# Bending the graph part with features on partitions: transposes in place of the second products

## The chip, the cores and the metric

The kernel runs on one core of a Trainium2 chip. The metric is device time in microseconds (us) from start to end of the program. An ordinary stretch of this kernel uses five engines at once: TensorE (products and transposes), VectorE, ScalarE, GpSimd and SyncE, which only issues transfers. They meet at semaphores. On-chip memory has 128 partitions. TensorE writes its results to a small separate memory (PSUM, here ps0 to ps7), from which VectorE and ScalarE read.

## The reference, cut to what matters

There are 6250 nodes with 256 features and 100,000 edges. The output is `x + gnn + mix` and a mixture-of-experts part on top. The change touches only the graph part (gnn), whose sums over edges are multiplied with W, shifted and scaled by statistics over all nodes and features, and bent with a leaky slope:

```python
xn = _layernorm(x, axis=-1)
# _L0_gnn_ref(xn, ...)
h = x @ W                                  # 6250 x 256 by 256 x 256
deg = jax.ops.segment_sum(jnp.ones_like(dst_f, dtype=h.dtype), dst_f, num_segments=n)
dinv = jax.lax.rsqrt(deg)
norm = dinv[src_f] * dinv[dst_f]
out = jax.ops.segment_sum(h[src_f] * norm[:, None], dst_f, num_segments=n) + conv_bias
mu = out.mean()
xc = out - mu
std = jnp.sqrt((xc * xc).mean())
y = xc / (std + EPS) * ln_weight + ln_bias
return jnp.where(y >= 0, y, prelu_a * y)
# then
x = x + gnn(xn) + mix(xn)
x = x + ffn(_layernorm(x, axis=-1))        # 8 experts, the best two of each row
```

## The kernel before

The program is a sequence of phases with a barrier behind each.

1. Statistics, degrees, a scaled table of rows in DRAM (to about 138 us).
2. Aggregation (140 to 789 us, groups `q` of edges). It sums table rows over edges with one-hot products, and runs the attention part between. The sums lie in `acc` with the 256 features on partitions (two halves `k` of 128) and the nodes along the row: `acc[:, k, node]`. At its end, SyncE loads the last weights (lines 725 to 731), and x tiles and table rows (lines 710, 716, 718) stand before them in its queue. `o_tile(t)` (in R2) holds x plus the attention result for tile t, features of both halves side by side, nodes on partitions.
3. The router phase (789 to 972 us), where the change lies. It works on T = 49 tiles of 128 nodes.
   - First pass: `rows(t)` on TensorE (line 1456) turns a tile of `acc` into 128 nodes by 256 features with two products by W (`gw`). VectorE scales it by `dinv` of each node and adds the bias (line 1615) and takes its statistics (1620).
   - Totals: VectorE joins the statistics (1639 to 1656) and asks TensorE twice for sums over partitions (1472, 1473). ScalarE takes a root (1536). VectorE multiplies W by the final scale of each feature (`wx`, line 1665).
   - Second pass: `scaled(t)` on TensorE (1482) repeats the two products, now by `wx`. VectorE scales by `dinv` and adds the shift (1675). ScalarE takes the negative part (1542), GpSimd adds the value into `o_tile` (1588). VectorE adds the negative part times 1 - slope (`finish`, 1681), and takes row statistics (1686, 1690). TensorE turns the finished tile (`flip`, 1491), ScalarE copies it (1548), TensorE multiplies it with the 8 router columns (`logits`, 1498).
   - Behind it, VectorE turns the statistics into scales (1704 to 1712) and chooses the experts (from 1724 on). ScalarE writes normalised rows (1564). One-hot products find each row's place (1526).
4. Experts (972 to 1377 us).

Each engine runs its own list in the order written. In the second pass TensorE's step s is `scaled(s)`, `flip(s - 4)`, `logits(s - 5)`; VectorE's is `shifted(s)`, `x_stats(s - 3)`, `x_stats_joined(s - 4)`, `finish(s - 2)`. SyncE stores each four finished tiles (`store_x1`, waits for `x_ok`) and loads expert weights over parts of `acc` that are done with (`load_w2`, waits for `px_ok`).

A float32 product is two instructions in the trace, a float32 transpose one.

Of the kernel before, what the change touches and what calls it, by code (L numbers as in the profile page):

```python
# [7 lines left out]
P = 128  # L8
# [47 lines left out]
W1ROW = KC * HID + HC  # L56


def build(nc, a_x, a_src, a_dst, a_gw, a_cb, a_lnw, a_lnb, a_pre, a_wqkv, a_mk, a_mv, a_wout, a_bout,
# [4 lines left out]
    ntable = nc.dram_tensor("ntable", (N, D + 2), f32, kind="Internal").ap()  # L64
    with ExitStack() as ctx:
# [34 lines left out]
        dslow = R1[:, 0:NC].rearrange("p (g c) -> p g c", c=GC)  # L100
        gw = RG[:, 4 * D:6 * D].rearrange("p (k n) -> p k n", k=KC)
        cbias, lnw, lnb = (RG[:, k * D:(k + 1) * D] for k in (6, 7, 8))
# [28 lines left out]
        pre = sb("pre", [P, 1])  # L131
        brr = sb("brr", [P, NX])
# [524 lines left out]
        with nc.Block(no_gpsimd_drain=True) as block:  # L657
# [43 lines left out]
            late = semaphore(phase, "a_late_weights_in")  # L701

            @block.sync
            def _(sp):
# [27 lines left out]

# [13 lines left out]
            def _(pe):  # L746
# [86 lines left out]
                def attention(q, r):  # L833
# [23 lines left out]
                    if q == C1 + 2 and r == 2:  # L857
                        pe.wait_ge(mid_dve, 5)
                        nc.tensor.matmul(psO, cnT, wout[:, :], start=True, stop=True).then_inc(mid_pe, 1)
                        pe.wait_ge(mid_dve, 6)  # L860
                    for s in quarter(share(q, B0, B1, T + 3), r):
# [102 lines left out]
            def _(v):  # L964
# [117 lines left out]
                def attention(q, r):  # L1082
# [61 lines left out]
                    if q == B1 + 1 and r == 0:  # L1144
# [6 lines left out]
                                                               ALU.mult))  # L1151
                    for t in quarter(share(q, D0, D1, T), r):
# [133 lines left out]
        aw, a1 = slot[:, 2, :], small[:, 20:21]  # L1286
        tot2, share_of = small[:, 24:26], small[:, 48:50]
        wx = RG[:, 0:2 * D].rearrange("p (k n) -> p k n", k=KC)
        bx = RG[:, 2 * D:3 * D]
# [61 lines left out]
        with nc.Block(no_gpsimd_drain=True) as block:  # L1351
            pr_ok = semaphore(phase, "r_products")
            y_ok = semaphore(phase, "r_rows_ready")
# [6 lines left out]
            sh_ok = semaphore(phase, "r_shares")  # L1360
            wx_ok = semaphore(phase, "r_scaled_weights")
            px_ok = semaphore(phase, "r_scaled_products")
            v_ok = semaphore(phase, "r_shifted")
            ng_ok = semaphore(phase, "r_negative_part")
# [698 lines left out]
```

## Time and profile before

| what | value |
|---|---|
| median of 3 runs | 1373.95 us |
| the three runs | 1378.43, 1372.21, 1373.95 us |
| profiled execution | span 1377.2 us from its first to its last instruction; its own time is not listed apart |
| TensorE, VectorE busy | 1245.3 us (90%), 962.4 us (70%) |
| ScalarE, GpSimd busy | 539.3 us (39%), 854.3 us (62%) |
| mean granted TensorE clock | 0.960 of full speed |

PE is TensorE's products and PEld its loads of the stationary operand, DVE is VectorE, ACT ScalarE, POOL GpSimd and SP SyncE. A `q` behind an engine's name is its sequencer. PEclk is the granted clock of TensorE as a share of 2.4 GHz: it has two levels, 0.50 and 1.00, and a value between is a stretch with both. A matmul's recorded duration contains its way through the array, so that the distance from start to start tells what it costs in a stream.

### The profile page before, as it was taken

Reading aid. Unit: us, or ns where it says so; the run is one execution under the profiler, and the core shown is the slowest. Engines: PE = TensorE matmul, PEld = TensorE weight load, DVE = VectorE, ACT = ScalarE, POOL = GpSimd, SP = SyncE. Lnnn points to the kernel's source line nnn. Section 1 sums busy time; section 2 is a strip of 40 time slices with the busy share of each in tenths; the row PEclk is TensorE's granted clock in tenths of the full one; section 3 lists DMA queues with packets and bytes.
Section 4 is the critical chain, followed back from the end, with each engine's and each line's share of the span. In section 5 each row is a group of like instructions: output and inputs, shape, how many; then the busy total and the mean of one; then the engine's idle time right before and its main releaser. Section 6 shows DMA issues by size and latency. Waiting matters only on the chain. (4 is left out here: it accounts for less than half of the span.)

```text
span 1377.2 us, 30864 instructions
## 1 busy us (share of the span) xinstructions
PE 1245.3 (90%) x8354; PEld 1106.3 (80%) x8355; DVE 962.4 (70%) x2966; ACT 539.3 (39%) x1443; POOL 854.3 (62%) x836
## 2 busy tenths in 40 slices
PE   4997688999899999999898797985799999999998
PEld 4984687887788888887787686873699999999997
DVE  8998787887888777778693288998444444444444
ACT  7707301222333333333311101446455555555553
POOL 1294677777777777777777202431376666666665
PEclk9999899999999999999999898995799999999999
DMA  7005333335666666789898400449244444444443
GB/s 245 0 0 183 111 106 103 107 105 172 194 194 199 198 191 202 207 246 277 260 288 261 144 1 16 138 155 318 64 77 66 68 71 69 72 69 70 71 69 42
DMA packets 138148, 186.89 MB, mean 136 GB/s; under 512 B 21438, under 2 KB 116468, under 8 KB 137916
## 3 DMA queue, kind: packets, MB, share of 16 engines
q0 software_dynamic: 43440, 90.29, 28.7%
q1 hardware_dynamic: 94604, 95.40, 21.8%
q8 instruction: 42, 0.69, 0.2%
q14 instruction: 62, 0.51, 0.1%
HBM read 153.16 MB, written 33.41 MB: 135 GB/s over the span
## 5 line engine op out<-in xcount | busy, mean ns | idle before, releaser
L740 POOL DMA_INDIRECT RG<-table,srci x484 | 477.3, 986 | 153.0 <-issue 149.4
L757 PEld LDWEIGHTS ps<-S_t,RG 128*128 128x128 f32 x1936 | 259.2, 196 | 39.0 <-DMA RG<-table,srci 28.6
L757 PE MATMUL ps<-S_t,RG 128*128 128x96 f32 x1936 | 266.4, 278 | 21.6 <-DMA RG<-table,srci 21.1
L780 PE MATMUL ps<-zrow,R 128*128 128x256 f32 (+1 forms) x784 | 221.1, 389 | 15.2 <-DMA zrow<-table 8.7
L2010 POOL DMA_INDIRECT out<-R,S_t x105 | 166.3, 1584 | 99.5 <-DVE R L1980 55.8
L1893 PE MATMUL ps<-R,RG 128*128 128x128 f32 x1680 | 207.3, 277 | 0.0
L1893 PEld LDWEIGHTS ps<-R,RG 128*128 128x128 f32 x1680 | 198.3, 194 | 0.4 <-issue 0.4
L1903 PE MATMUL ps<-R 128*128 x840 | 198.5, 379 | 0.0
L1014 DVE TENSOR_TENSOR R<-R,ps 128x245 f32 (+4 forms) x300 | 142.1, 474 | 73.7 <-PE ps L768 52.5
L1926 ACT ACTIVATE R<-ps,RG 128x128 f32<-128x128 f32 x420 | 120.0, 368 | 175.8 <-PE ps L1893 175.8
L1976 DVE TENSOR_TENSOR R<-ps,R 128x256 f32<-128x256 f32 x105 | 44.6, 425 | 200.8 <-PE ps L1903 200.8
L780 PEld LDWEIGHTS ps<-zrow,R 128*128 128x128 f32 (+1 forms) x784 | 136.9, 192 | 41.2 <-DMA zrow<-table 19.8
L1903 PEld LDWEIGHTS ps<-R 128*128 128x128 f32 x840 | 151.7, 190 | 16.3
L884 ACT ACTIVATE R<-iwin 128x256 f32<-128x256 f32 (+2 forms) x152 | 71.3, 476 | 186.0 <-PE ps L780 174.2
L1998 POOL DMA_INDIRECT R<-ntable,S_t x105 | 104.2, 992 | 41.5 <-issue 29.0
L1935 ACT ACTIVATE RG<-R 128x1028 f32 x105 | 112.8, 1076 | 10.6 <-PEq L76 10.6
L1588 POOL TENSOR_TENSOR R<-R,slot 128x256 f32<-128x256 f32 x49 | 35.9, 733 | 93.5 <-DVE slot L1675 93.5
L455 PE MATMUL ps<-R 128*128 128x49 bf16 x784 | 80.7, 276 | 10.4 <-DVE R L544 10.3
L455 PEld LDWEIGHTS ps<-R 128*128 128x128 bf16 x784 | 72.7, 144 | 18.4 <-DVE R L544 12.2
L1965 DVE TENSOR_SCALAR R<-ps,gamma,beta 128x128 f32<-128x128 f32 x212 | 76.1, 400 | 0.0
L971 DVE TENSOR_TENSOR S_t<-dstrel,iwin 128x384 f32<-128x384 f32 x121 | 66.7, 551 | 0.7
L984 DVE TENSOR_TENSOR R<-R,ps 128x192 f32 x121 | 42.7, 353 | 31.0 <-issue 23.4
(360 smaller groups left out, 1989.9 us busy)
## 6 DMA issues: line engine op xcount, KB each, us to landing
zrow<-table SPq DMA_DIRECT2D x384, 128.0 KB
RG<-table,srci POOLq DMA_INDIRECT x484, 3.3
ntable<-R SPq DMA_DIRECT2D x12, 516.0 KB
table<-RG SPq DMA_DIRECT2D x12, 512.0 KB, 2.9
out<-R SPq DMA_DIRECT2D x12, 512.0 KB, 3.2
R<-in_x SPq DMA_DIRECT2D x6, 896.0 KB, 11.7
R<-in_w SPq DMA_DIRECT2D x8, 514.0 KB, 6.4
slot<-in_x SPq DMA_DIRECT2D x32, 128.0 KB
```

Source lines behind the costliest of these rows:

```text
L455: last = nc.tensor.matmul(ps[7][:, 0:T], ohlo[k][:, :, c], ohhi[k][:, :, c], start=False, stop=False)
L740: nc.gpsimd.indirect_dma_start(out=grows[:, s, :], out_offset=None, in_=table, in_offset=bass.IndirectOffsetOnAxis(ap=srci[:, ND + q, c:c ...
L757: last = nc.tensor.matmul(window(q % 2)[:, h, :], grows[:, s, h * P:(h + 1) * P], S_t[:, q % 2, c, :], start=c == 0, stop=c == GC - 1)
L780: nc.tensor.matmul(psD[:, 0:D], adj[b % 2][0:n, j, :], zrow[0:n, i % ZR, :], start=j == 0, stop=j == T - 1).then_inc(z_used, 1)
L1014: nc.vector.tensor_tensor(win, win, psK[m % 2][:, 0:T * wide].rearrange("p (j w) -> p j w", w=wide), ALU.add).then_inc(cnt_ok, 1)
L1893: last = nc.tensor.matmul(psH[s % 2][:, h * P:(h + 1) * P], w1r[:, s, k * HID + h * P:k * HID + (h + 1) * P], ur[:, s % 2, k, :], start=k ...
L1903: last = nc.tensor.matmul(psY[s % 2][:, 0:D], hr[:, s % 2, h, :], w2_sb[:, bass.ds(e, 1), h, :].rearrange("p a f -> p (a f)"), start=h == ...
L1926: last = act.activation(hr[:, s % 2, h, :], psH[s % 2][:, h * P:(h + 1) * P], ACT.Gelu, bias=w1r[:, s, KC * HID + h:KC * HID + h + 1])
L1935: act.activation(w1r[:, s, :], w1_sb[:, bass.ds(e, 1), :].rearrange("p a f -> p (a f)"), ACT.Copy).then_inc(c_ok, 1)
L1965: nc.vector.tensor_scalar(ur[:, s % 2, k, :], psX[s % 2][:, k * P:(k + 1) * P], gamma[:, k:k + 1], beta[:, k:k + 1], ALU.mult, ALU.add)
L1998: nc.gpsimd.indirect_dma_start(out=xr[:, t % 4, :], out_offset=None, in_=ntable, in_offset=bass.IndirectOffsetOnAxis(ap=gat[:, t:t + 1], a ...
L2010: nc.gpsimd.indirect_dma_start(out=a_out, out_offset=bass.IndirectOffsetOnAxis(ap=sct[:, t:t + 1], axis=0), in_=yr[:, t % 4, :], in_offset ...
```

## The change

The order of work behind the aggregation is turned round. W is applied once, in the form that leaves the features on partitions, and the value that comes out replaces the sums in `acc`.

- The row of all `dinv` is needed on every partition. TensorE transposes `dinv` late in the aggregation, it is stored to DRAM as `dflat` (25 KB), and one transfer spreads it to `dall`, 128 partitions of 25,000 bytes each (3.2 MB). It may be issued once the seventh block has been turned, since `dall` lies over that block's counts.
- First pass: `features(i)`, 26 pieces (13 spans of 500 nodes, the last of 250, by 2 halves of the features), each of two products with W stationary and the sums moving. VectorE multiplies each by `dall` back into `acc` and takes statistics of each 250 nodes.
- Bias, weight and shift are now a number per partition, loaded as 2 numbers per partition each (three small transfers), instead of rows of 256 spread over the partitions.
- Second pass, in 13 slabs of 512 nodes: ScalarE scales and shifts the lower half in place (`affine`), VectorE bends it with one instruction (`bent`). For the upper half ScalarE makes two slabs, the line with the small slope (`steep`) and the rectified rest, and GpSimd adds them. `back(t)` transposes the tile to nodes on partitions, and `finish(t)` on VectorE adds it to `o_tile(t)` straight from PSUM. The per-tile work of ScalarE and GpSimd of before (1542, 1588), `shifted` (1675) and the joining of row statistics (1690) are gone; the latter is done for all tiles at once behind the pass. `flip` and `logits` stay, two steps behind instead of four.

```diff
@@ -722,13 +735,19 @@
...
+                    if q == B1 + 6:
+                        sp.wait_ge(dr_ok, 1)
+                        sp.dma_start(dflat.rearrange("(t p) -> t p", p=P), ksl[0:T, 0, :]).then_inc(dr_out, 16)
+                sp.wait_ge(dr_out, 16)
+                sp.wait_ge(blk_t, NDB - 1)
+                sp.dma_start(dall, dflat[0:N].unsqueeze(0).to_broadcast([P, N])).then_inc(da_in, 16)
                 sp.wait_ge(pe_done, GQ - 2)
                 sp.dma_start(gw, a_gw.rearrange("(k p) n -> p k n", p=P)).then_inc(late, 16)
-                sp.dma_start(cbias, a_cb.unsqueeze(0).to_broadcast([P, D])).then_inc(late, 16)
-                sp.dma_start(lnw, a_lnw.unsqueeze(0).to_broadcast([P, D])).then_inc(late, 16)
-                sp.wait_ge(pe_done, GQ - 1)
-                sp.dma_start(lnb, a_lnb.unsqueeze(0).to_broadcast([P, D])).then_inc(late, 16)
+                for dest, source in ((cbf, a_cb), (lnwf, a_lnw), (lnbf, a_lnb)):
+                    sp.dma_start(dest[:, :], source.rearrange("(k p) -> p k", p=P),
+                                 allow_slow_non_contiguous=True).then_inc(late, 16)
                 sp.wait_ge(late, 16 * 4)
+                sp.wait_ge(da_in, 16)
...
@@ -1449,38 +1473,42 @@
...
-                def rows(t):
-                    if t >= 4:
-                        pe.wait_ge(y_ok, t - 3)
+                def features(i):
+
+                    j, f = i // KC, i % KC
+                    if i >= 6:
+                        pe.wait_ge(u_ok, i - 5)
+                    lo, hi = j * SPAN, min(j * SPAN + SPAN, N)
                     for k in range(KC):
-                        last = nc.tensor.matmul(ps[t % 4][:, 0:D], acc[:, k, t * P:(t + 1) * P], gw[:, k, :],
+                        last = nc.tensor.matmul(ps[i % 6][:, 0:hi - lo], gw[:, k, f * P:(f + 1) * P], acc[:, k, lo:hi],
                                                 start=k == 0, stop=k == KC - 1)
                     last.then_inc(pr_ok, 1)
 
-                for t in range(4):
-                    rows(t)
+                for i in range(4):
+                    features(i)
                 pe.wait_ge(g_ok, 2)
                 for k in range(KC):
-                    nc.tensor.matmul(ps[5][:, 0:NX], betas[:, k, :], wr[:, k, :], start=k == 0, stop=k == KC - 1)
+                    nc.tensor.matmul(ps[6][:, 0:NX], betas[:, k, :], wr[:, k, :], start=k == 0, stop=k == KC - 1)
                 for k in range(KC):
-                    last = nc.tensor.matmul(ps[6][:, 0:NX], ones[:, :], wrg[:, k, :], start=k == 0, stop=k == KC - 1)
+                    last = nc.tensor.matmul(ps[7][:, 0:NX], ones[:, :], wrg[:, k, :], start=k == 0, stop=k == KC - 1)
                 last.then_inc(g_ps, 1)
-                for t in range(4, T):
-                    rows(t)
+                for i in range(4, KC * NSPAN):
+                    features(i)
                 for n in range(2):
                     pe.wait_ge(part, n + 1)
-                    nc.tensor.matmul(ps[7][:, n:n + 1], ones[:, :], tot2[:, 0:1], start=True, stop=False)
-                    nc.tensor.matmul(ps[7][:, n:n + 1], ones[:, :], tot2[:, 1:2], start=False,
-                                     stop=True).then_inc(whole, 1)
-
-                pe.wait_ge(wx_ok, 1)
-
-                def scaled(t):
+                    for k in range(KC):
+                        last = nc.tensor.matmul(ps[7][:, n:n + 1], ones[:, :], tot2[:, k:k + 1], start=k == 0,
+                                                stop=k == KC - 1)
+                    last.then_inc(whole, 1)
...
+                def back(t):
+                    pe.wait_ge(pr_in, t // 4 + 1)
+                    pe.wait_ge(ps_in, t // 4 + 1)
                     if t >= 2:
-                        pe.wait_ge(v_ok, t - 1)
+                        pe.wait_ge(x_ok, t - 1)
                     for k in range(KC):
-                        last = nc.tensor.matmul(psW[t % 2][:, 0:D], acc[:, k, t * P:(t + 1) * P], wx[:, k, :],
-                                                start=k == 0, stop=k == KC - 1)
+                        last = nc.tensor.transpose(psW[t % 2][:, k * P:(k + 1) * P], acc[:, k, t * P:(t + 1) * P],
+                                                   ident[:, :])
                     last.then_inc(px_ok, 1)
...
@@ -1499,13 +1527,13 @@
...
-                for s in range(T + 5):
+                for s in range(T + 3):
                     if s < T:
-                        scaled(s)
-                    if 0 <= s - 4 < T:
-                        flip(s - 4)
-                    if 0 <= s - 5 < T:
-                        logits(s - 5)
+                        back(s)
+                    if 0 <= s - 2 < T:
+                        flip(s - 2)
+                    if 0 <= s - 3 < T:
+                        logits(s - 3)
...
@@ -1535,11 +1563,17 @@
...
-                def negative(t):
-                    act.wait_ge(v_ok, t + 1)
-                    if t >= 4:
-                        act.wait_ge(x_ok, t - 3)
-                    act.activation(minus[:, t % 4, :], shift[:, t % 4, :], ACT.Relu, scale=-1.0).then_inc(ng_ok, 1)
+                def affine(c):
+                    lo, hi = c * SLAB, min(c * SLAB + SLAB, NP)
+                    act.activation(acc[:, 0, lo:hi], acc[:, 0, lo:hi], ACT.Identity, scale=aw[:, 0:1],
+                                   bias=bw[:, 0:1]).then_inc(af_ok, 1)
+                    if c >= 2:
+                        act.wait_ge(ps_in, c - 1)
+                    act.activation(steep[:, c % 2, 0:hi - lo], acc[:, 1, lo:hi], ACT.Identity, scale=down[:, 0:1],
+                                   bias=down[:, 1:2]).then_inc(lf_ok, 1)
+                    act.wait_ge(lf_ok, c + 1)
+                    act.activation(acc[:, 1, lo:hi], acc[:, 1, lo:hi], ACT.Relu, scale=kink[:, 0:1],
+                                   bias=kink[:, 1:2]).then_inc(kn_ok, 1)
...
@@ -1547,11 +1581,13 @@
...
+                act.wait_ge(fn_ok, 1)
+                for c in range(2):
+                    affine(c)
+                for t in range(T):
+                    if t % 4 == 0 and t // 4 + 2 < NSLAB:
+                        affine(t // 4 + 2)
+                    flipped(t)
...
@@ -1575,20 +1611,17 @@
...
-                def residual(t):
-                    pool.wait_ge(v_ok, t + 1)
-                    nc.gpsimd.tensor_tensor(o_tile(t), o_tile(t), halved(shift[:, t % 4, :]), ALU.add).then_inc(xa_ok, 1)
-
-                for t in range(T):
-                    residual(t)
+                for c in range(NSLAB):
+                    lo, hi = c * SLAB, min(c * SLAB + SLAB, NP)
+                    pool.wait_ge(kn_ok, c + 1)
+                    nc.gpsimd.tensor_tensor(acc[:, 1, lo:hi], acc[:, 1, lo:hi], steep[:, c % 2, 0:hi - lo],
+                                            ALU.add).then_inc(ps_in, 1)
...
@@ -1610,49 +1643,54 @@
...
+                def scaled(j):
+                    lo, hi = j * SPAN, min(j * SPAN + SPAN, N)
+                    v.wait_ge(pr_ok, KC * j + KC)
+                    for f in range(KC):
+                        nc.vector.tensor_tensor(acc[:, f, lo:hi], ps[(KC * j + f) % 6][:, 0:hi - lo], dall[:, lo:hi],
+                                                ALU.mult).then_inc(u_ok, 1)
+
+                def feature_stats(j):
+                    v.wait_ge(u_ok, KC * j + KC)
+                    for f in range(KC):
+                        for i in range(2 * j, min(2 * j + 2, NPIECE)):
+                            last = nc.vector.bn_stats(fstats[:, f, i, :], acc[:, f, i * PIECE:(i + 1) * PIECE])
+                    return last
...
+                for k in range(KC):
+                    last = nc.vector.bn_aggr(both[:, k, :], fstats[:, k, :, :].rearrange("p i s -> p (i s)"))
+                ch.done(last)
+                ch.done(nc.vector.tensor_tensor(tot2, means, cbf[:, :], ALU.add))
...
@@ -1661,46 +1699,48 @@
...
+                ch.done(nc.vector.tensor_tensor(d2, d2, side, ALU.mult))
+                ch.done(nc.vector.tensor_scalar(aw, lnwf[:, :], d2, None, ALU.mult))
+                ch.done(nc.vector.scalar_tensor_tensor(bw, cbf[:, :], mu, aw, ALU.subtract, ALU.mult))
+                ch.done(nc.vector.scalar_tensor_tensor(bw, lnbf[:, :], side, bw, ALU.mult, ALU.add))
+                nc.vector.tensor_tensor(down[:, 0:1], aw[:, 1:2], pre[:, :], ALU.mult)
+                nc.vector.tensor_tensor(down[:, 1:2], bw[:, 1:2], pre[:, :], ALU.mult)
+                nc.vector.tensor_tensor(kink[:, 0:1], aw[:, 1:2], kink[:, 2:3], ALU.mult)
+                ch.done(nc.vector.tensor_tensor(kink[:, 1:2], bw[:, 1:2], kink[:, 2:3], ALU.mult))
+                v.sem_inc(fn_ok, 1)
...
+                def bent(c):
+                    lo, hi = c * SLAB, min(c * SLAB + SLAB, NP)
+                    v.wait_ge(af_ok, c + 1)
+                    nc.vector.scalar_tensor_tensor(acc[:, 0, lo:hi], acc[:, 0, lo:hi], pre[:, 0:1], acc[:, 0, lo:hi],
+                                                   ALU.mult, ALU.max).then_inc(pr_in, 1)
...
+                def finish(t):
                     v.wait_ge(px_ok, t + 1)
-                    if t >= 4:
-                        v.wait_ge(ng_ok, t - 3)
-                        v.wait_ge(xa_ok, t - 3)
-                    nc.vector.scalar_tensor_tensor(shift[:, t % 4, :], psW[t % 2][:, 0:D], dinv[:, t:t + 1], bx, ALU.mult,
-                                                   ALU.add).then_inc(v_ok, 1)
-
-                def finish(t):
-                    v.wait_ge(ng_ok, t + 1)
-                    v.wait_ge(xa_ok, t + 1)
-                    nc.vector.scalar_tensor_tensor(halved(o_all[:, t, :]), halved(minus[:, t % 4, :]), a1, o_tile(t),
+                    nc.vector.scalar_tensor_tensor(halved(o_all[:, t, :]), halved(psW[t % 2][:, 0:D]), side, o_tile(t),
                                                    ALU.mult, ALU.add).then_inc(x_ok, 1)
...
-                def x_stats_joined(t):
-                    v.wait_ge(st_ok, t + 1)
-                    nc.vector.bn_aggr(mv[:, t, :], stats[:, t, :]).then_inc(ag_ok, 1)
...
+                bent(0)
+                for s in range(T + 1):
+                    if s % 4 == 0 and s // 4 + 1 < NSLAB:
+                        bent(s // 4 + 1)
                     if s < T:
-                        shifted(s)
-                    if 0 <= s - 3 < T:
-                        x_stats(s - 3)
-                    if 0 <= s - 4 < T:
-                        x_stats_joined(s - 4)
-                    if 0 <= s - 2 < T:
-                        finish(s - 2)
-                v.wait_ge(ag_ok, T)
-                mean, var = mv[:, :, 0], mv[:, :, 1]
-
+                        finish(s)
+                    if 0 <= s - 1 < T:
+                        x_stats(s - 1)
...
```

On TensorE, around the first pass and the totals in front of the second. `ps` is PSUM, `R` the large buffers (`acc` and the rows), `RG` the weights, `small` a tile of scalars. Before:

```order
L1456 MATMUL ps<-RG,R 128x256 x8
L1464 MATMUL ps<-wr,RG 128x8 x2
L1466 MATMUL ps<-RG,ones 128x8 x2
L1456 MATMUL ps<-RG,R 128x256 x90
L1472 MATMUL ps<-small,ones 128x1
```

After:

```order
L1483 MATMUL ps<-R,RG 128x500 x8
L1491 MATMUL ps<-wr,RG 128x8 x2
L1493 MATMUL ps<-RG,ones 128x8 x2
L1483 MATMUL ps<-R,RG 128x500 x40
L1483 MATMUL ps<-R,RG 128x250 x4
L1500 MATMUL ps<-small,ones 128x1 x4
```

98 products of 256 columns have become 48 of 500 and 4 of 250.

On TensorE in the second pass, from its first instruction on. Before:

```order
L1482 MATMUL ps<-RG,R 128x256 x10
L1491 MATMUL ps<-ident,R 128x128 x2
L1482 MATMUL ps<-RG,R 128x256 x2
L1491 MATMUL ps<-ident,R 128x128 x2
L1498 MATMUL ps<-RG,zrow 128x8 x2
L1482 MATMUL ps<-RG,R 128x256 x2
L1491 MATMUL ps<-ident,R 128x128 x2
L1498 MATMUL ps<-RG,zrow 128x8 x2
```

After:

```order
L1510 MATMUL ps<-ident,R 128x128 x6
L1519 MATMUL ps<-ident,R 128x128 x2
L1510 MATMUL ps<-ident,R 128x128 x2
L1519 MATMUL ps<-ident,R 128x128 x2
L1526 MATMUL ps<-RG,zrow 128x8 x2
L1510 MATMUL ps<-ident,R 128x128 x2
L1519 MATMUL ps<-ident,R 128x128 x2
L1526 MATMUL ps<-RG,zrow 128x8 x2
```

Of a tile's two wide products, two transposes and two narrow products, the wide ones have become transposes.

On ScalarE after, from the first slab on (`zrow` is the turned tile, `slot` the slab `steep`):

```order
L1568 ACTIVATE R<-R,small 128x512
L1572 ACTIVATE slot<-R,small 128x512
L1575 ACTIVATE R<-R,small 128x512
L1568 ACTIVATE R<-R,small 128x512
L1572 ACTIVATE slot<-R,small 128x512
L1575 ACTIVATE R<-R,small 128x512
L1568 ACTIVATE R<-R,small 128x512
L1572 ACTIVATE slot<-R,small 128x512
L1575 ACTIVATE R<-R,small 128x512
L1582 ACTIVATE zrow<-ps 128x256 x4
L1568 ACTIVATE R<-R,small 128x512
```

Three wide instructions now stand in front of each four copies of turned tiles, where before one narrow instruction stood in front of each copy.

## Rows read from the trace of the kernel before

**Rows 1.** The page: TensorE's busy tenths and granted clock in 40 slices.

```profile
PE   4997688999899999999898797985799999999998
...
PEclk9999899999999999999999898995799999999999
```

**Rows 2.** Windows of the router phase: length, busy us by engine, clock, DMA.

```profile
790.00:836.00 46.00, 45.95 (x204) 39.77 (x204) 39.52 (x101) 1.59 (x1) 1.47 (x7) 0.94 0.00 1
...
845.00:920.00 75.00, 74.38 (x462) 66.09 (x463) 71.54 (x186) 32.04 (x92) 35.16 (x48) 0.97 0.36 113
```

**Rows 3.** Timeline of TensorE in the second pass, one tile (start, us, line).

```profile
917.90 0.38 PE L1491 MATMUL ps<-ident,R 128*128 128x128 f32 x2
918.12 0.51 PE L1498 MATMUL ps<-RG,zrow 128*128 128x8 f32 x4
918.49 1.11 PE L1482 MATMUL ps<-RG,R 128*128 128x256 f32 x4
919.43 0.38 PE L1491 MATMUL ps<-ident,R 128*128 128x128 f32 x2
```

**Rows 4.** Timeline of TensorE elsewhere, at the lower clock.

```profile
841.04 0.59 PE L1472 MATMUL ps<-small,ones 128*128 128x1 f32 x2 [1.23 <-DVEq L1652]
841.49 0.56 PE L1473 MATMUL ps<-small,ones 128*128 128x1 f32 x2
...
980.99 0.64 PE L1883 MATMUL ps<-ident,R 128*128 128x128 f32 x2
981.42 2.66 PE L1893 MATMUL ps<-R,RG 128*128 128x128 f32 x16
```

**Rows 5.** Windows where the clock falls, stays low, and rises.

```profile
842.00:844.00 2.00, 0.05 (x1) 0.00 (x0) 1.38 (x8) 0.20 (x1) 0.00 (x0) 0.50 0.00 0
...
850.00:852.00 2.00, 2.00 (x12) 1.68 (x11) 1.89 (x5) 0.84 (x2) 1.32 (x2) 1.00 0.00 0
...
924.00:926.00 2.00, 0.61 (x4) 0.52 (x4) 1.50 (x6) 0.24 (x1) 0.00 (x0) 0.72 1.07 246
...
955.00:960.00 5.00, 5.00 (x27) 3.32 (x24) 4.71 (x6) 3.35 (x8) 1.95 (x2) 0.50 1.05 370
```

**Rows 6.** Timeline: totals, start of the second pass, and its end.

```profile
832.76 3.19 PE L1456 MATMUL ps<-RG,R 128*128 128x256 f32 x14
...
836.39 0.74 DVE L1620 BATCH_NORM_STATS2 RG<-R 128x6 f32<-128x256 f32 x2
837.16 1.45 DVE L1639 BATCH_NORM_AGGREGATE small<-RG 128x2 f32<-128x288 f32 x1
...
844.74 6.66 PEld L1482 LDWEIGHTS ps<-RG,R 128*128 128x128 f32 x20 [2.77 <-DVEq L1666]
...
922.58 0.45 DVE L1681 SCALAR_TENSOR_TENSOR R<-zrow,small,R 128x256 f32<-128x256 f32 x1
...
926.12 0.57 DVE L1724 TENSOR_TENSOR R<-ps,zs_s 128x392 f32<-128x392 f32 x1
```

**Rows 7.** Groups by line: first pass, second pass, wide ScalarE instructions.

```profile
L1615 DVE SCALAR_TENSOR_TENSOR R<-ps,dinv,RG 128x256 f32<-128x256 f32 x49 | 23.7, 483 | 6.4 <-PE ps L1456 4.6
...
L1588 POOL TENSOR_TENSOR R<-R,slot 128x256 f32<-128x256 f32 x48 | 35.2, 733 | 92.7 <-DVE slot L1675 92.7
...
L1935 ACT ACTIVATE RG<-R 128x1028 f32 x105 | 112.8, 1076 | 10.6 <-PEq L76 10.6
L1564 ACT ACTIVATE R<-R,zs_b,zs_s 128x256 f32<-128x256 f32 x49 | 24.8, 588 | 11.4 <-DMA ntable<-R 9.6 <-DVEq L1713 1.8
```

**Rows 8.** Timeline at the end of the aggregation: SyncE's issues, what waits.

```profile
771.34 0.29 SPq L718 DMA_DIRECT2D slot<-in_x  x1
776.82 0.38 SPq L726 DMA_DIRECT2D RG<-in_gw  x1
...
777.66 0.60 ACT L920 ACTIVATE slot<-slot,x1b,x1s 128x256 f32<-128x256 f32 x1 [1.40 <-DMA slot<-in_x]
...
786.06 0.36 DVE L984 TENSOR_TENSOR R<-R,ps 128x192 f32 x1 [2.61 <-PE ps L757]
```

More of the change, by code:

```diff
@@ L131, in build @@
         pre = sb("pre", [P, 1])
+        cbf, lnwf, lnbf = (RG[:, 16 * D + KC * k:16 * D + KC * (k + 1)] for k in range(3))
         brr = sb("brr", [P, NX])
@@ L860, in attention @@
                         pe.wait_ge(mid_dve, 6)
+                    if q == B1 + 1 and r == 0:
+                        pe.wait_ge(qt_ok, T)
+                        nc.tensor.transpose(psT[0:T, :], dinv[:, :], ident[:, :]).then_inc(mid_pe, 1)
                     for s in quarter(share(q, B0, B1, T + 3), r):
@@ new lines, in feature_stats @@
+                def feature_stats(j):
[4 more added lines that the diff above has]
+                    return last
+                scaled(0)
+                for j in range(NSPAN):
+                    if j + 1 < NSPAN:
+                        scaled(j + 1)
+                    if j == 2:
@@ L1627, in _ @@
                         v.wait_ge(g_ps, 1)
-                        ch.done(nc.vector.tensor_tensor(c0, ps[5][:, 0:NX], brr[:, :], ALU.add))
+                        ch.done(nc.vector.tensor_tensor(c0, ps[6][:, 0:NX], brr[:, :], ALU.add))
                         for k in range(KC):
-                            last = nc.vector.scalar_tensor_tensor(wrg[:, k, :], ps[6][:, 0:NX], -1.0 / D, wrg[:, k, :],
+                            last = nc.vector.scalar_tensor_tensor(wrg[:, k, :], ps[7][:, 0:NX], -1.0 / D, wrg[:, k, :],
@@ L1631, in _ @@
                                                                   ALU.mult, ALU.add)
                         ch.done(last)
-                    last = row_stats(t)
+                    last = feature_stats(j)
                 ch.done(last)
-                full = 1.0 / (N * D)
-                pm, tm = small[:, 32:34], small[:, 34:36]
-                means, variances = (small[:, 32:36].rearrange("p (a b) -> p a b", b=2)[:, :, k] for k in range(2))
-                ch.done(nc.vector.bn_aggr(pm, stats[:, 0:T - 1, :].rearrange("p t s -> p (t s)")))
@@ L1640, in _ @@
-                ch.done(nc.vector.bn_aggr(tm, stats[:, T - 1, :]))
-                v.wait_ge(sh_ok, 2)
-                ch.done(nc.vector.tensor_tensor(tot2, means, share_of, ALU.mult))
+                both = small[:, 32:32 + 2 * KC].rearrange("p (k s) -> p k s", s=2)
+                means, variances = both[:, :, 0], both[:, :, 1]
+                for k in range(KC):
+                    last = nc.vector.bn_aggr(both[:, k, :], fstats[:, k, :, :].rearrange("p i s -> p (i s)"))
+                ch.done(last)
@@ L1651, in _ @@
-                ch.done(nc.vector.tensor_tensor(tot2, off, share_of, ALU.mult))
+                ch.done(nc.vector.tensor_tensor(tot2, off, variances, ALU.add))
                 v.sem_inc(part, 1)
@@ L1654, in _ @@
                 val, root = small[:, 31:32], small[:, 30:31]
-                ch.done(nc.vector.tensor_scalar(val, ps[7][:, 1:2], full, 1e-30, ALU.mult, ALU.max))
+                ch.done(nc.vector.tensor_scalar(val, ps[7][:, 1:2], 1.0 / D, 1e-30, ALU.mult, ALU.max))
                 v.sem_inc(root_in, 1)
```

88 lines of the change are left out of this document (43 added, 45 removed).

## The prediction

> **What bounds the kernel now.** I read the page first, from its clock and busy lines: TensorE is busy nearly everywhere, at full clock but for a few dents, the deep one in slices 28 and 29, right behind the passes that the change rewrites (slices 24 to 27) [rows 1]. Then windows by stage. In the first pass of the router phase (790 to 836) TensorE is busy without a break and VectorE for 39.5 of 46 us; in the second (845 to 920) both are full, 74.4 and 71.5 of 75 us [rows 2]. Then TensorE's timeline of one tile in the second pass: a transpose pair to the next pair takes 917.90 to 919.43, 1.53 us, and its parts fill it: 0.22 for two transposes, 0.37 for the narrow products, 0.94 for the wide ones [rows 3]. So both passes hang on TensorE, and their sum is 46 + 78.3 us (844.74 to 922.58 + 0.45, the last `finish`) [rows 6].
>
> The view that decides this case is the clock. TensorE's clock was at 0.50 after the gap (842 to 844), and rose to 1.00 by 850 to 852 under the first twenty 256-column products of the second pass. It fell again in 924 to 926, when the engine had done only transposes and narrow products for the last tiles. And it stayed at 0.50 through 955 to 960, though TensorE was busy 5.00 of 5.00 us with a stream of 105-column bf16 products [rows 5]. Being occupied did not raise it there; wide float32 products did.
>
> **Second pass, the largest term.** The change takes away the wide products, 0.94 us of the 1.53, and puts two transposes there. At full clock a tile is 0.22 + 0.22 + 0.37 = 0.81 us [rows 3]. But the gap before the pass grows: ScalarE and GpSimd must make a slab first, so TensorE stands for some 14 us behind the first pass and starts at 0.50. What it then gets is the very mix that was in front of the fall, transposes and 8-column products, with nothing wide to raise the clock. I expect it to stay at 0.50 for the whole pass. Twice 0.81 is 1.62 us. The rows at 0.50 say directly: two transposes 0.43 (980.99 to 981.42), two narrow instructions 0.45 (841.04 to 841.49), so at most 0.86 + 0.90 = 1.76 [rows 4]. I take 1.65, near the doubled value, because the narrow ones in rows 4 hold a first start; bounds 1.60 and 1.76. 49 x 1.65 = 80.9 us.
>
> Start: ScalarE's 512-column instruction does not occur before. 256 columns with two scalars per partition take 0.588, 1028 plain ones 1.076 [rows 7]; so 512 lie between 0.588 + 256 x (1.076 - 0.588) / 772 = 0.75 and 2 x 0.588 = 1.18. I take 0.8, since the longer row shows how little a column adds. The three of a slab overlap a little, the third waits for the second: 2.4 us to its end. GpSimd's add of 512 is between 0.73 and 1.47 (256 take 0.733 [rows 7]); 1.4. So the first transposes come at 4.0 us after VectorE's flag, where the first wide product now comes at once. The third step waits for the first `finish`, 0.6. Behind the last `back` stand three flips and four sets of narrow products, 3 x 0.43 + 4 x 0.79 = 4.4 us, that the last `finish` does not wait for; transposes and `finish` themselves end 0.9 later. From flag to last `finish`: 4.0 + 0.6 + 80.9 - 4.4 + 0.9 = 82.0 against 78.3: **+3.7 us**, with the bounds of the tile -2.5 and +5.4 around it.
>
> What that hides: VectorE has per four tiles four `finish` (0.48 each by the like L1615 [rows 7]), four statistics (0.37 each by L1620 [rows 6]) and one `bent` of 512, below twice 0.75 even beside GpSimd: under 5 us of 6.6. GpSimd has 1.4 of 6.6. The 98 small instructions taken from ScalarE and GpSimd and the 49 joins on VectorE were beside TensorE and bring nothing. ScalarE is the close one: a slab's three instructions stand in front of each fourth copy, and TensorE cannot pass that copy by more than a step. The circle is slab 2.3, copy 0.37, narrow products 0.8, a whole step 1.65, a `back` and a `flip` 0.86, latencies 0.5: 6.5 us per four tiles against TensorE's 6.6. If TensorE were quicker, this circle would be the bound.
>
> **First pass.** 196 instructions of 256 columns become 96 of 500 and 8 of 250. Fourteen took 3.19 us with the last one's 0.38 [rows 6], so 0.216 apart; 500 columns take 0.42. 41.7 instead of 42.3: -0.6. VectorE has 2 x 0.6 + 4 x 0.34 = 2.6 us per span against TensorE's 3.4, so it stays hidden until the last span. Behind the last product there are now two scalings of 250 and six statistics, 2 x 0.35 + 6 x 0.34 = 2.75, against 1.2 (835.95 to 837.13): +1.6. Joining: 1.45 for 288 values and 0.2 become two of 150 at the same rate, 1.5: -0.15 [rows 6]. Of the small steps behind, the product of W by the scale (0.7) goes and six steps of 0.1 to 0.2 come: 0, within 0.4. **+0.85 us.**
>
> **End of the pass.** Now 3.1 us from the last `finish` to the first step of the choice (923.03 to 926.12 [rows 6]). Joining all statistics at once adds five dependent steps of about 0.25 between them: **+1.2 us**. The last narrow products end 4.0 us behind `finish`, just inside.
>
> **End of the aggregation.** `dall` can be issued right behind the last x tile, at 771.6. 3.2 MB at the 370 GB/s of the busiest window [rows 5] are 8.6 us. The x tile issued at 771.34 landed at 777.66 [rows 8], so some transfer path is late; the part of `dall` behind it would land at 786.3, the weights behind that near 787.5. VectorE's last add ends the phase at 786.42 now [rows 8]. I take **+1.0 us**: hidden altogether is 0, and every transfer in single file about +4. The transpose, the copy and the 25 KB store at group 89 to 94 are nothing beside a whole group's work there.
>
> **Sum.** 3.7 + 0.85 + 1.2 + 1.0 = +6.75 us. The profiled execution's span was 1377.2, inside the three runs (1372.21 to 1378.43); the difference is carried over to their median: 1373.95 + 6.75 = 1380.7, so 1381. A change of 0.5%, 6.9 us, is what I take a measurement to tell from none; the forecast lies on that border.
>
> **Rival 1: the clock comes up.** Then ScalarE's circle binds: 2.3 + 0.37 + 0.4 + 0.81 + 0.43 + 0.4 = 4.7 us, 1.2 per tile. 4.0 + 0.6 + 49 x 1.2 - 2.2 + 0.7 = 61.9, -16.4 against 78.3, with the other terms -13.3: 1361. For it: in 845 to 920 transposes and narrow products ran at full clock between wide ones [rows 2]. Against: rows 5, twice.
> The Trainium skill, TensorE: Matmul & The Clock Gate, section What's actually happening, says that the throttled state is the default and activity releases it, by how busy the engine has been; by that rule TensorE, occupied without a break at 1.65 us per tile, would be released. The trace disagrees in 955 to 960, occupied for 5.00 us at 0.50; 0.16 is what I leave to the rule.
>
> **Rival 2: ScalarE's slabs take TensorE's place.** With 1.18 per wide instruction a slab is 3.4, the circle 7.6 per four tiles, 1.9 per tile: 49 x 0.25 = +12: 1393. It decides from 0.83 per instruction on. For it: two scalars per partition cost at 256 columns more than a plain instruction. Against: 1028 columns in 1.076.
>
> **Rival 3: `dall` and what stands behind it end the aggregation**, about 3 us later than I took: 1384, slower.
>
> **How the numbers follow.** Forecast 0.70, its own range 1376 to 1387, split by the border at 1380.8 into 0.34 below and 0.36 above. Rival 1 0.16 (faster). Rival 2 0.08, rival 3 0.06 (slower). Faster 0.16, same 0.34, slower 0.50. A range of 1373 to 1391 leaves out rival 1 and half of rival 2.
>
> **What would show it.** Right: PEclk 0.50 from the gap to the experts; 1.6 to 1.75 us from pair to pair of `back`; TensorE waiting little, ScalarE less than full; a first transpose 4 us behind the flag; the first pass within a microsecond of its length. Rival 1: PEclk 1.00 in the pass and 1.2 us per tile, TensorE waiting for line 1582. Rival 2: the same wait at 0.50, and line 1568 at 1.1 us. Rival 3: SyncE's last wait ending the aggregation. The forecast is wrong if the clock rises under transposes and narrow products alone, or if transposes at 0.50 run other than 0.21 apart.

## The result, and the profile after

The changed kernel took 1384.62 us (median of 7 runs, 1381.17 to 1386.80) against 1373.95 for the kernel before (7 runs, 1371.16 to 1381.38): ratio 1.0070, 95% interval 1.0049 to 1.0091, so slower by 0.5 to 0.9%. (A ratio is worked out from the single runs of both kernels, so it is not exactly the quotient of the two medians.) The forecast was 1381, 1373 to 1391, slower the likeliest of the three.

The page of the changed kernel, the lines of [rows 1]:

```profile
PE   4997688999899999998898696995799999999998
...
PEclk9999898999999999999999896555799999999999
```

The dent in the clock was two slices long (5, 7) and is now five (6, 5, 5, 5, 7). Above it TensorE reads 6 in the gap and then 9, 9. Windows of the router phase in the changed kernel (columns as in [rows 2]): the first pass, the gap, the second pass.

```profile
791.00:836.00 45.00, 44.69 (x112) 21.05 (x112) 29.82 (x72) 1.61 (x1) 1.30 (x5) 0.96 0.00 0
836.00:851.00 15.00, 2.32 (x10) 2.18 (x11) 9.80 (x36) 4.12 (x7) 1.09 (x1) 0.59 0.00 1
851.00:928.00 77.00, 76.51 (x374) 73.98 (x372) 47.53 (x108) 40.39 (x80) 12.40 (x12) 0.50 0.35 112
```

TensorE stands for most of 15 us, its clock falls, and in the second pass it is busy for 76.51 of 77 us at 0.50. VectorE, full there before, has 30 us to spare. One tile of the second pass, TensorE's timeline of the changed kernel, against [rows 3]:

```profile
902.66 0.67 PE L1510 MATMUL ps<-ident,R 128*128 128x128 f32 x2
903.12 0.64 PE L1519 MATMUL ps<-ident,R 128*128 128x128 f32 x2
903.55 0.86 PE L1526 MATMUL ps<-RG,zrow 128*128 128x8 f32 x4
904.26 0.67 PE L1510 MATMUL ps<-ident,R 128*128 128x128 f32 x2
```

902.66 to 904.26 is 1.60 us. As long as slabs are made, each fourth tile takes 1.76, since the narrow product waits for ScalarE's copy behind a slab. The start and the end of the second pass, VectorE's timeline of the changed kernel, against [rows 6] (L1709 is the step ahead of the flag, L1720 `finish`, L1764 the first step of the choice):

```profile
846.77 0.15 DVE L1709 TENSOR_TENSOR small<-small 128x1 f32<-128x1 f32 x1
...
851.40 0.91 DVE L1720 SCALAR_TENSOR_TENSOR R<-ps,small,R 128x256 f32<-128x256 f32 x2 [0.30 <-PE ps L1510]
...
927.71 0.48 DVE L1720 SCALAR_TENSOR_TENSOR R<-ps,small,R 128x256 f32<-128x256 f32 x1 [0.78 <-PE ps L1510]
...
932.85 0.57 DVE L1764 TENSOR_TENSOR R<-ps,zs_s 128x392 f32<-128x392 f32 x1
```

And the end of the aggregation, against [rows 8]: VectorE's last add and its wait for the next phase, then SyncE's issues, then the DMA view (KB, us from issue to landing).

```profile
785.79 0.36 DVE L1006 TENSOR_TENSOR R<-R,ps 128x192 f32 x1 [1.42 <-PE ps L776]
790.95 0.72 DVE L1641 TENSOR_SCALAR RG<-wr,gamma 128x8 f32<-128x8 f32 x2 [4.81 <-PEq L84]
```

```profile
771.01 0.40 SPq L743 DMA_DIRECT2D R<-dflat  x1
...
778.76 0.49 SPq L747 DMA_DIRECT2D RG<-in_lnb  x1
```

```profile
R<-dflat SPq DMA_DIRECT2D x1, 3125.0 KB, 15.1
...
RG<-in_lnb SPq DMA_DIRECT2D x1, 1.0 KB, 8.5
```

The last 1 KB load lands at 778.76 + 8.5 = 787.3, 1.1 us behind the last add's end.

### The profile page after: what moved, and what is told of

Read it like the earlier page. It is cut to its first block and busy times, and to the rows that moved or that the text cites. A ratio compares the mean times of both kernels' runs of the same rounds, so it can differ in the third digit from the quotient of the medians.

```text
span 1384.0 us, 30256 instructions
## 1 busy us (share of the span) xinstructions
PE 1244.8 (90%) x8165; PEld 1098.6 (79%) x8166; DVE 931.8 (67%) x2872; ACT 550.3 (40%) x1433; POOL 827.3 (60%) x798
## 5 line engine op out<-in xcount | busy, mean ns | idle before, releaser
L1623 POOL TENSOR_TENSOR R<-R,slot 128x512 f32<-128x512 f32 (+1 forms) x13 | 13.5, 1038 | 113.2 <-ACT R L1575 113.2
L553 DVE TENSOR_TENSOR R<-R,RG 128x1792 bf16<-128x1792 bf16 x56 | 62.6, 1119 | 0.7 <-DVE flag_i L546 0.3
```

## The experiments

Every ratio is to the kernel before, run on the same chip; the changed kernel's is 1.0070. "Filling" means float32 products whose results nobody reads:

```diff
+                def fill(n, wide=512):
+                    for _ in range(n):
+                        nc.tensor.matmul(ps[6][:, 0:wide], ones[:, :], gwide[:, 0:wide], start=True, stop=True)
+                fill(12)
                 for n in range(2):
...
                     last.then_inc(whole, 1)
+                    fill((2, 13)[n])
```

**Gap filled, too long.** 

> The changed kernel with float32 products of 512 columns put where TensorE would stand ahead of the second pass: 12 behind the first pass, 2 between the two totals, 13 behind the second. Nobody reads their results. Theory: the second pass runs at 0.50 because TensorE stood ahead of it and nothing wide follows. Then the pass starts here at 1.00, and either holds it (1.2 us per tile, about 1365 us) or falls within some tiles (1.6 us per tile again, 1382 to 1385 us, at most 2 us better than the changed kernel). I take the second: the kernel before lost the clock at 924 to 926 us behind transposes and narrow products alone. Rival, ScalarE's slabs bind the pass: no change from the start at 1.00, 1.6 us per tile at either clock, 1384 us with the clock at 1.00.

1389.15 us, ratio 1.0087 (1.0059 to 1.0115). The clock did what I expected, it fell within the pass; the time was a miss: each product is two instructions of 0.43 us, and I had filled the gap twice over. TensorE's timeline (of the kernel that also holds, where it is the same):

```profile
836.47 10.46 PE L1500 MATMUL ps<-RG,ones 128*128 128x512 f32 x24
```

Where the clock fell shows more than the time. TensorE's timeline of this kernel, 7 us into the pass, and its windows:

```profile
862.80 0.38 PE L1526 MATMUL ps<-ident,R 128*128 128x128 f32 x2
864.50 1.02 PE L1533 MATMUL ps<-RG,zrow 128*128 128x8 f32 x4 [1.32 <-ACT zrow L1589]
```

```profile
860.00:864.00 4.00, 3.18 (x30) 2.94 (x29) 4.00 (x12) 2.80 (x5) 0.00 (x0) 1.00 0.41 135
864.00:868.00 4.00, 3.50 (x18) 3.50 (x18) 1.80 (x5) 1.11 (x4) 1.36 (x1) 0.56 0.82 261
```

Eight tiles' transposes ran at 1.00. Then TensorE stood 1.32 us for the copy that ScalarE makes behind a slab, and was at 0.50 from there to the end of the pass.

**Gap filled and the clock held.**

```diff
                         logits(s - 3)
+                    if s < T:
+                        fill(1, 128)
```

> As the one with the filled gap, and in each tile of the second pass one more float32 product of 128 columns, not read by anybody. Theory (the clock is what the pass pays): the clock stays at 1.00 through the pass. TensorE's own work is then 0.81 + 0.22 = 1.03 us per tile, and ScalarE's circle of a slab and a copy binds at 1.2: 49 x (1.63 - 1.2) = 21 us less than the changed kernel, 1363 us, and ahead of the kernel before. Rival, ScalarE or the slabs bind already at 1.6 us per tile: no gain, 1384. Rival, the narrow mix pulls the clock down all the same: 1.6 + 0.4 = 2.0 us per tile, some 1403.

1376.46 us, ratio 1.0006 (0.9990 to 1.0022); the window of the pass:

```profile
862.00:922.00 60.00, 52.96 (x458) 50.72 (x457) 51.45 (x104) 36.78 (x76) 10.25 (x10) 1.00 0.44 141
```

The clock holds, and `finish` to `finish` is 1.27 us (48 tiles from 860.96 to 922.08), close to the 1.2 of ScalarE's circle; TensorE waits in nine places. The other two outcomes are out. The 1.2 is a mean: most groups of four tiles hold one wait of 0.78 us. Of the 13.5 us missing to the expected 1363, 9 are the overlong filling and 49 x 0.07 = 3.4 the tile.

**The slab's three instructions apart.**

```diff
-                    if t % 4 == 0 and t // 4 + 2 < NSLAB:
-                        affine(t // 4 + 2)
+                    if t % 4 < 3 and t // 4 + 2 < NSLAB:
+                        affine(t // 4 + 2, t % 4)    # one of the three instructions
```

> As the one with the filled gap and the 128-column product per tile, and ScalarE's three instructions of a slab stand in front of three tiles, one each, in place of together in front of each fourth. If at 1.00 the slabs in one piece are what sets 1.2 us per tile, this brings the tile down to TensorE's 1.03 to 1.1 us, 5 to 8 us less than with the slabs together: about 1357. If the slabs are not what sets it, the two take the same time.

1367.66 us, ratio 0.9933 (0.9910 to 0.9957), 8.8 us below the one with the slabs together. The window of its pass:

```profile
862.00:912.00 50.00, 50.00 (x455) 49.95 (x452) 43.18 (x105) 38.75 (x78) 11.37 (x11) 1.00 0.53 169
```

TensorE waits for nothing and a tile takes 1.08 us on the mean. So at 1.00 the slabs in one piece set the pace, as expected. The expected 1357 was missed by 10.7 us, since it started from the 1363 that the kernel with the slabs together did not reach.

**The same without filling.** 

> The changed kernel with only the spreading of ScalarE's three slab instructions over three tiles; no added products. Theory: at a clock of 0.50 TensorE sets the tile (1.60 us), and each fourth takes 1.76 because a narrow product waits for the copy behind the slab: at most 12 x 0.16 = 2 us less, 1383. Rival, ScalarE's slabs have taken TensorE's place as the bound: spreading frees ScalarE in front of each fourth copy, and a tile falls well below 1.6 us, 1375 or less.

Eleven of twelve executions took 1376.2 to 1384.9 us at a mean clock of 0.927 to 0.933; their median, 1380.68, is 1.0040 of the kernel before. One took 1347.18 at a mean clock of 0.957. An interval for this ratio would say little, since the two groups of times belong to one kernel. The trace is of one of the eleven; TensorE's timeline and the window:

```profile
901.01 0.67 PE L1510 MATMUL ps<-ident,R 128*128 128x128 f32 x2
...
902.62 0.67 PE L1510 MATMUL ps<-ident,R 128*128 128x128 f32 x2
```

```profile
853.00:925.00 72.00, 71.76 (x359) 71.37 (x358) 44.82 (x104) 39.72 (x79) 12.45 (x12) 0.50 0.37 117
```

Every tile is 1.60 us, the 1.76 are gone, and from the first `finish` to the last it is 74.7 us in place of 76.8: 2.1, as expected. Of the 4 us between the medians I can place only these. At 0.50 TensorE is the bound, not ScalarE.

**Held only, gap empty** (the 128-column product per tile, nothing else). 

> The changed kernel with one float32 product of 128 columns more in each tile of the second pass, not read by anybody, and nothing in the gap ahead of the pass. Theory: the pass starts at 0.50, and transposes, 8-column products and now 128 columns of a product are still too little to raise the clock; TensorE's tile is 1.63 + 2 x 0.22 = 2.07 us, 21 us more than the changed kernel, about 1405. Rival, an engine that is occupied is released, or this product is wide enough: the clock rises within the pass, the tile is then 1.1 to 1.3 us, and the time lies at 1365 to 1372.

1370.74 us, ratio 0.9951 (0.9935 to 0.9966). My theory missed by 34 us and the rival is right. Windows of this kernel:

```profile
845.00:850.00 5.00, 0.00 (x0) 0.00 (x0) 2.35 (x12) 3.19 (x5) 0.78 (x1) 0.50 0.00 0
850.00:853.00 3.00, 2.54 (x12) 2.57 (x13) 2.30 (x5) 2.93 (x5) 1.41 (x2) 0.50 0.00 0
853.00:914.00 61.00, 53.95 (x464) 51.52 (x463) 52.11 (x105) 37.70 (x78) 11.33 (x11) 1.00 0.44 141
```

With one product of 128 columns for each tile among the transposes, the clock rose 2.8 us into the pass. The first 8-column product stands behind the rise, at 853.97 us: what raised the clock was transposes and 128-column products alone, and no run shows whether the full mix with narrow products would have. The waits behind the slabs are there (TensorE busy 53.95 of 61, nine waits, none above 0.79 us) and did not bring it down.

**The kernel before with its gap filled** (3, 1 and 2 products of 512). 

> The kernel before the change with six unread float32 products of 512 columns in its gap: 3 behind the first pass, 1 between the totals, 2 behind the second. Its second pass ran at 0.50 for its first 5 to 7 us. Theory: with the gap filled it starts at 1.00 and ends 2.5 to 3 us earlier: about 1372.5, ratio 0.998. Rival, those first microseconds wait for VectorE and not for the clock: no change.

1372.79 us, ratio 0.9982 (0.9969 to 0.9995): 2.5 us by the ratio, as expected. In the traces VectorE's way from the flag to the last `finish` is 2.4 us shorter, 76.0 in place of 78.4. The window over the start of its second pass, and the same stretch of the kernel before:

```profile
840.00:850.00 10.00, 9.23 (x50) 7.74 (x51) 8.81 (x23) 3.73 (x10) 5.23 (x7) 1.00 0.05 17
```

```profile
842.00:852.00 10.00, 7.31 (x24) 5.93 (x24) 5.77 (x17) 1.87 (x5) 2.78 (x4) 0.61 0.01 2
```

So filling alone is worth 0.2% to the kernel before. What the filled versions of the changed kernel gain beyond that comes from the change and, where they are spread, from the order of ScalarE's instructions.

**Filling of the right length** (6, 1, 7; held and spread). 

> The kernel of the filled gap, the product of 128 columns per tile and the spread slabs, with the gap filled no longer than it lasts: 6, 1 and 7 products of 512 columns in place of 12, 2 and 13, which took 0.87 us each and held the first total up by 4.9 us, the second by 0.3 and the first transposes by 4.2. Theory: these 9 us come off, with the clock at 1.00 through the pass and 1.08 us per tile: 1367.7 - 9 = 1359, ratio 0.988. Rival, TensorE stands too long with the shorter filling and the clock falls: 1380 to 1385.

1358.63 us, ratio 0.9869 (0.9847 to 0.9891), as expected. In its trace TensorE is busy 52.79 of the 53 us from 849 to 902, at 1.00, and a tile takes 1.08 us.

**The same without the product per tile.** 

> Gap filled as in the sized one and slabs spread, but no product of 128 columns in the tiles. Theory: the pass starts at 1.00 and falls after some 6 tiles, as with the slabs together (864.5 us, 7 us into the pass); then 1.60 us per tile: 6 tiles at 0.5 us less, 1377 to 1380. Rival, transposes and 8-column products alone hold the clock where ScalarE does not hold TensorE up (one execution of the kernel with only the slabs spread took 1347 us at a mean clock of 0.957, the other eleven 1376 to 1385 at 0.93): 1.08 us per tile or less, 1350 to 1359.

1346.39 us, ratio 0.9793 (0.9773 to 0.9814). The theory missed by 32 us. The rival is right about the clock, and the time lies 4 us below its range. The page, the window of the pass and TensorE's timeline of a tile:

```profile
PE   4998688999899999999988879966999999999998
...
PEclk9999798999999999999999979975899999999999
```

```profile
847.00:889.00 42.00, 41.51 (x377) 39.72 (x375) 41.91 (x109) 37.55 (x81) 12.44 (x12) 1.00 0.64 201
```

```profile
872.36 0.42 PE L1517 MATMUL ps<-ident,R 128*128 128x128 f32 x2
872.61 0.38 PE L1526 MATMUL ps<-ident,R 128*128 128x128 f32 x2
872.83 0.51 PE L1533 MATMUL ps<-RG,zrow 128*128 128x8 f32 x4
873.20 0.41 PE L1517 MATMUL ps<-ident,R 128*128 128x128 f32 x2
```

The same instructions for a tile as in the changed kernel, 0.84 us for this tile and 0.86 over the pass. VectorE, busy 41.91 of 42 us, now bounds the pass as closely as TensorE with 41.51. This is the fastest version, 38 us below the changed kernel.

**The same with the slabs together.** 

> The changed kernel with the sized filling of the gap alone (6, 1 and 7 unread products of 512 columns), slabs together in front of each fourth copy. Theory: the pass starts at 1.00 and the clock falls at the first stand of TensorE behind a slab (1.32 us in the kernel with the long filling, and the clock fell as it ended), then stays at 0.50: 1.6 us per tile but for the first six to eight, 1379 to 1382. Rival, the spreading adds nothing and the mix holds the clock in any order: 1.2 us per tile, 1360 to 1364.

1379.55 us, ratio 1.0035 (1.0014 to 1.0055), as expected: TensorE's first stand behind a slab, and the windows on both sides of the fall:

```profile
849.42 0.38 PE L1526 MATMUL ps<-ident,R 128*128 128x128 f32 x2
851.17 0.61 PE L1533 MATMUL ps<-RG,zrow 128*128 128x8 f32 x4 [1.37 <-ACT zrow L1589]
```

```profile
847.00:853.40 6.40, 4.09 (x34) 3.51 (x34) 5.57 (x13) 4.96 (x10) 3.03 (x3) 1.00 0.25 82
853.40:923.00 69.60, 69.41 (x341) 67.44 (x341) 42.20 (x96) 36.27 (x73) 10.24 (x10) 0.50 0.37 115
```

Up to this stand TensorE's timeline is that of the spread kernel, step for step. So the order of three ScalarE instructions decides over 33 us here, though the longest wait that it takes away is 1.4 us: it decides whether the clock stays. The pair does not tell whether the length of this one stand counts or how much TensorE stands in the stretch around it (busy 4.09 of 6.40 us ahead of the fall).

**Only the last part of the filling.** 

> Slabs spread, and only the last part of the filling: 7 unread products of 512 columns behind the second total, none behind the first pass and between the totals. The clock falls in the first part of the gap, as it does in the changed kernel. Theory: wide products right ahead of the pass raise it again, and the transposes and 8-column products only have to hold it: 0.87 us per tile, but the first products take twice as long at 0.50 and may delay the first transposes by up to 4 us: 1346 to 1351. Rival, the clock has to be held through the whole gap: 1.60 us per tile, 1380 to 1385.

1350.76 us, ratio 0.9823 (0.9801 to 0.9845), as expected. Its windows: the gap, the filling at the lower clock, the filling at the higher one, and the pass.

```profile
837.00:844.00 7.00, 2.82 (x9) 2.28 (x10) 4.52 (x17) 0.20 (x1) 0.00 (x0) 0.55 0.00 1
844.00:848.00 4.00, 4.00 (x6) 1.69 (x5) 2.52 (x13) 1.83 (x3) 0.00 (x0) 0.50 0.00 0
848.00:851.50 3.50, 3.50 (x9) 1.48 (x8) 0.98 (x1) 3.44 (x5) 1.75 (x2) 1.00 0.00 0
851.50:892.00 40.50, 40.01 (x361) 38.17 (x360) 39.99 (x103) 35.23 (x77) 11.76 (x12) 1.00 0.65 206
```

Wide products right ahead of the pass raise the clock, and the pass only keeps it. The clock need not be kept through the gap.

**An eighth of `dall`.** 

> The changed kernel with the load of dall cut to its first eighth (390 KB in place of 3125), which leaves the output wrong in the columns behind it; everything else is as before. It is read at the end of the aggregation. Theory: the whole load (15.1 us from issue to landing) and the small ones behind it were what ended that phase, 787.3 us, 1.1 us behind VectorE's last add. With an eighth they land by 783 to 785 and VectorE's last add ends the phase: VectorE stands 3.5 to 3.8 us ahead of its first scaling of W in place of 4.8, as before the change, and the whole time is 1.0 us less than the changed kernel. Rival, the 1 KB loads are late by themselves: 4.8 us as in the changed kernel.

1382.59 us, ratio 1.0061 (1.0041 to 1.0081): too close to 1.0070 for the time to tell. The trace tells; VectorE ahead of the first pass, and the loads:

```profile
784.55 0.72 DVE L1641 TENSOR_SCALAR RG<-wr,gamma 128x8 f32<-128x8 f32 x2 [3.51 <-PEq L84]
```

```profile
R<-dflat SPq DMA_DIRECT2D x1, 390.5 KB, 7.2
...
RG<-in_lnb SPq DMA_DIRECT2D x1, 1.0 KB, 2.2
```

The small loads take 2.2 us in place of 8.5 when the large one ahead of them is small, and VectorE stands 3.51 us in place of 4.81.

## Why the prediction was right, and where it was not

The profiled executions differ by 1384.0 - 1377.2 = 6.8 us; the sum was 6.75. The four terms below make 6.7 before rounding, and 0.1 comes behind the choice. That the sums agree this well is luck in part: 0.8 us too many in the second pass stand against 0.8 too few in two other terms. Term by term:

| Term | foretold | measured in the trace |
|---|---|---|
| End of the aggregation | +1.0 | +1.0 (790.95 - 789.92) |
| First pass | +0.85 | +1.3 (56.0 to the flag, 54.7 before) |
| Second pass | +3.7 | +2.9 (flag 846.92 to 928.19, 81.3 against 78.4) |
| End of the pass | +1.2 | +1.6 (928.19 to 932.85, 4.66 against 3.09) |

- **The second pass** was right in each part that it was built of: the clock at 0.50 from the gap to the experts, the first transposes 3.8 us behind the flag (4.0 foretold), 1.63 us per tile (1.65 taken), ScalarE at 0.80 per instruction (0.8 taken). GpSimd's add was priced too high, 1.09 against 1.4. Most of the 0.8 us too many are small terms at the ends: 0.2 at the first transposes, 0.24 in place of 0.6 for the third step's wait, and 0.7 in place of 0.9 behind the last transposes. TensorE from its first transposes to its last narrow product takes 81.2 us (850.71 to 931.95), against 0.6 + 80.9 foretold.
- **The end of the aggregation** came by the mechanism that was named, a queue of small loads behind `dall`: VectorE stands 1.3 us longer, and its last add ends 0.3 us earlier. The shortened load gives the 1.3 us back. Rival 3's further 3 us did not come.
- **First pass and end of the pass** are each 0.4 us over. VectorE's tail, two scalings and six statistics behind the last product, is 2.7 us (836.50 to 839.16) and the joining 1.5, both as foretold; what remains of the first pass is in the small dependent steps behind them, 0.4 in place of 0. At the end of the pass seven new steps stand in place of the five counted (1.4 us, 928.88 to 930.28), and the wait for ScalarE's root is 0.2 longer. VectorE's timeline of the changed kernel:

```profile
836.50 0.73 DVE L1650 TENSOR_TENSOR R<-ps,R 128x250 f32<-128x250 f32 x2
837.15 2.01 DVE L1657 BATCH_NORM_STATS2 RG<-R 128x6 f32<-128x250 f32 x6
839.19 1.52 DVE L1677 BATCH_NORM_AGGREGATE small<-RG 128x2 f32<-128x150 f32 x2
```

- **The 0.6 us that the products of the first pass were to save** were summed wrongly, and came about by luck. At the 0.216 us per 256 columns that the prediction used, the new products take 42.2 us and not 41.7, 0.1 less than before. The stretch from the first product to VectorE's last scalings did become 0.5 us shorter (790.94 to 836.50 against 789.92 to 835.99), because only its first 3.4 us ran at 0.50, where it was 5.3 before: that difference alone is worth 0.9.
- **The reason for the clock was half right.** The step "what it then gets is the very mix that was in front of the fall" took the mix to be unable to keep the clock as well as unable to raise it. The second holds: 77 us of it in the changed kernel did not raise it. The first does not: at 1.00 the same mix kept it through 42 us where nothing made TensorE stand. [Rows 5] at 924 to 926 showed TensorE busy 0.61 of 2 us: the clock fell at 924.9, 0.3 us after TensorE had run out of work. So this row could not bear what the mix does while it runs without a stand. What made the clock fall just there stays open; the stands in front of it, from 920 us on, were 0.46 us and twice 0.13, and in the spread kernel with the filled gap the clock stayed at 1.00 for another 2.7 us after TensorE's last narrow product.
- **Rival 1 was priced wrong.** I took the clock and ScalarE's circle as two limits of which one binds, 1361 us. They are tied: at 1.00 the circle makes TensorE wait 1.3 us, and with that wait the 1.00 ends. The kernel with the gap filled and the slabs together, 1379.55, shows it. With the slabs apart the price of a full clock is 0.86 us per tile and not 1.2.
- **Rival 2** is out: at 0.50 ScalarE's slabs add 0.16 us to each fourth tile and no more.

The Trainium skill, TensorE: Matmul & The Clock Gate, section What's actually happening, has the throttled state released by how busy the engine has been. By the rule as I read it, 76.51 of 77 us busy would have been released; the trace disagrees. What lifted the clock here was a change in what TensorE did, not in how long: transposes with one product of 128 columns per tile did it within 3 us, at 2.54 of 3.00 us busy.

The medians differ by 10.7 us, 3.9 more than the traces. The kernel before was profiled in one of its longer executions (by the span of 1377.2 most likely the one of 1378.43 us; the seven lie at 1371.16 to 1381.38), the changed one near its median (1385.72), and I carried the difference of one execution over to the median unchanged. That step is where the 3.6 us between 1381 and 1384.62 lie; what makes one execution of the kernel before 4.5 us longer than another stays open. Open too is what raised the clock in that one execution of twelve, since its trace was not taken: its time and mean clock are those of a pass at 1.00.

## What to carry to other kernels

A clock level is a state, so ask two things of each stretch, what it enters with and whether it keeps it: the same 49 tiles took 1.63 us each or 0.86 by what TensorE did in the gap ahead of them and by one wait of 1.3 us within. When a change takes away wide products and opens a gap, count its gain at the lower clock, and try what unread wide products right ahead of the stage, and helpers' work spread evenly within it, give. Fill such a gap only as long as it lasts: in the held and spread kernel 9 us too many halved the gain (ratio 0.9933 against 0.9869). Give the kernel before the same filling too, so that its worth is not booked to the change: there it was 0.2%.

## What the runs showed of the hardware

- Transposes and 8-column float32 products kept 1.00 for 42 us in which TensorE stood for 0.5, and stayed at 0.50 for 77 us with hardly any. A stand of 1.32 or 1.37 us in the same mix was followed by 0.50 both times, at once in one kernel and 2.3 us later in the other; with a 128-column product per tile, nine stands of 0.78 us were not. No run has a stand above 0.8 us with that product, so whether it would bear 1.3 us is not shown.
- One kernel, whose pass was at 0.50 in the trace that was taken, gave times 33 us apart, 1347 once and 1381 as the median of the eleven others.
- Three 1 KB loads behind a load of 3125 KB landed after 5.0 to 8.5 us, behind one of 390 KB after 2.2 to 2.5.
- VectorE's 512-column `bent` took 0.75 us alone and 1.30 where GpSimd's add on a slab ran beside it for 0.75 us. Where the two met for 0.44 us it took 0.99, for 0.3 us (most slabs) 0.84: it became longer by the time that they met, less some 0.2 us:

```profile
854.33 1.30 DVE L1715 SCALAR_TENSOR_TENSOR R<-R,pre 128x512 f32<-128x512 f32 x1
```
